# Attention of a two-layer graph network: the gathers' lead over the products is limited to three groups

## The reference, cut to what matters

```python
h = (x @ W.T).reshape(n, H, D)
h_src, h_dst = h[src], h[dst]
alpha = einsum(h_src, a_src) + einsum(h_dst, a_dst)
enc = relu(edge_attr @ edge_W.T + edge_b).reshape(-1, H, D)
alpha = alpha + sum(enc * h_dst, axis=-1)
alpha = where(alpha >= 0, alpha, 0.2 * alpha)
ex = exp(alpha - segment_max(alpha, dst)[dst])
attn = ex / max(segment_sum(ex, dst)[dst], 1e-10)
out = segment_sum(h_src * attn[..., None], dst)
```

## Time and profile before

| | us |
|---|---|
| median of three runs | 3056.0 |
| profiled execution, whole | 3057.23 |
| its span, first to last instruction | 3055.5 |
| attention, from the first gather to the last sum | about 914 (1668 to 2582) |
| POOL busy with L1934 in all | 489.5 in 488 gathers |
| TensorE's mean granted clock | 0.826 of full |

### The profile page before, as it was taken

One profiled execution on the slowest core, in us unless ns is written; L12 is line 12 of the kernel. 1 busy time (PEld: TensorE's weight loads), 2 busy tenths in 40 slices (PEclk: granted clock), 3 DMA queues, 4 the chain that ended last, 5 costly groups with the idle time before them and its releaser, 6 DMA issues. The chain is left out here.

```text
span 3055.5 us, 41553 instructions
## 1 busy us (share of the span) xinstructions
PE 2069.6 (68%) x12602; PEld 1559.8 (51%) x12602; DVE 1660.6 (54%) x3320; ACT 817.5 (27%) x2162; POOL 1225.6 (40%) x1222
## 2 busy tenths in 40 slices
PE   3355656555549985899424276777776676996995
PEld 1244444434437764799412155555555554335995
DVE  7344444444447778555566276767776667403222
ACT  6222222222200001233123122323332323432331
POOL 0366666666640000455213455556565651001221
PEclk9677677777769997899756688888888888997998
DMA  2344444444358844222322344444444432300113
GB/s 74 106 153 153 151 153 152 157 151 147 139 167 296 293 166 137 87 72 71 92 87 83 83 120 117 123 115 132 121 127 117 128 112 78 126 9 20 39 36 104
DMA packets 192123, 366.16 MB, mean 120 GB/s; under 512 B 47573, under 2 KB 102632, under 8 KB 191525
## 3 DMA queue, kind: packets, MB, share of 16 engines
q1 hardware_dynamic: 135472, 207.05, 21.0%
q0 software_dynamic: 56160, 156.43, 16.6%
q10 hardware_dynamic: 274, 0.00, 0.0%
HBM read 232.23 MB, written 131.07 MB: 119 GB/s over the span
## 5 line engine op out<-in xcount | busy, mean ns | idle before, releaser
L1934 POOL DMA_INDIRECT att_rows<-hdram,top_ix x488 | 489.5, 1003 | 382.2 <-DVE att_msg L2162 231.0
L756 POOL DMA_INDIRECT mtab<-msgs_rw,msgs_ix x488 | 486.0, 996 | 376.9 <-ACT msgs_rw L718 186.0
L645 PE MATMUL msgs_p_m<-nodes_n,msgs_hott 128*128 x976 | 358.9, 530 | 54.6 <-issue 41.1
L2006 PE MATMUL att_p_acc<-att_msg,att_hot 128*128 128x264 f32 x976 | 307.5, 469 | 94.6 <-issue 45.0
L578 DVE TENSOR_TENSOR msgs_rw<-msgs_p_m,msgs_sorted 128x1024 f32<-128x1024 f32 x122 | 149.3, 1224 | 339.0 <-PE msgs_p_m L645 124.8
L645 PEld LDWEIGHTS msgs_p_m<-nodes_n,msgs_hott 128*128 128x128 f32 x976 | 245.4, 264 | 120.5 <-issue 75.3
L2006 PEld LDWEIGHTS att_p_acc<-att_msg,att_hot 128*128 128x128 f32 x976 | 211.2, 227 | 150.2 <-issue 89.4
L2036 ACT ACTIVATE att_enc<-att_p_z 128x1024 f32<-128x1024 f32 x122 | 124.8, 1023 | 592.2 <-remote 327.1
L2113 DVE TENSOR_TENSOR att_enc<-att_enc,att_p_h 128x1024 f32<-128x1024 f32 x122 | 148.8, 1220 | 242.6 <-remote 210.2
L826 PE MATMUL sums_part<-sums_rows,sums_hot 128*128 128x256 f32 x976 | 223.8, 387 | 32.4 <-DVE sums_hot L801 32.2
L1348 PE MATMUL exp_y<-exp_own,exp_ht 128*128 128x256 f32 x1032 | 239.0, 379 | 2.4 <-issue 2.4
(11 more groups left out here) (376 smaller groups left out, 3576.2 us busy)
## 6 DMA issues: line engine op xcount, KB each, us to landing
sums_rows<-mtab SPq DMA_DIRECT2D x122, 520.0 KB, 4.6
etab<-msgs_et SPq DMA_DIRECT2D x122, 288.0 KB
att_hz<-etab SPq DMA_DIRECT2D x122, 288.0 KB
first_w<-in_L_ffn_w SPq DMA_DIRECT2D x16, 512.0 KB
ffn0x_w<-in_L_ffn_w SPq DMA_DIRECT2D x16, 512.0 KB
ffn_w<-in_L_ffn_Wd SPq DMA_DIRECT2D x8, 1024.0 KB, 10.6
mtab<-msgs_rw,msgs_ix POOLq DMA_INDIRECT x488
att_rows<-hdram,top_ix POOLq DMA_INDIRECT x488
```

Source lines behind the costliest of these rows:

```text
L645: last = T.matmul(p_m[g % 2][:, q, :], hott[g % 2][:, q, :], node, start=True, stop=True)
L756: nc.gpsimd.indirect_dma_start(mtab, bass.IndirectOffsetOnAxis(ap=ix[:, g, q:q + 1], axis=0), rw[g % RS][:, q, :], None).then_inc(s_free[g ...
L1934: nc.gpsimd.indirect_dma_start(rows[:, g % RS, q, :], None, hdram, bass.IndirectOffsetOnAxis(ap=ix1[:, g, q:q + 1], axis=0)).then_inc(s_ro ...
L2006: last = T.matmul(p_acc[g % 2][:, 0:HW], hot[g % 2][:, q, :], msg[g % 2][:, q, :], start=(q == 0), stop=(q == G - 1))
```

## The change

POOL waits for DVE as well. Before the gathers of group g >= 3 it waits until `products` of group g - 3 has run (`s_prod` is counted up by line 2113), so group g's gathers are issued no earlier than after product g - 3. The wait for the ring slot stays as it was. The unused count `s_go` goes up from g = 3 on instead of from g = 12 on.

```diff
             for g in range(NG):
                 if g >= RS:
                     pool.wait_ge(s_msg, g - RS + 1)
+                if g >= 3:
+                    pool.wait_ge(s_prod, g - 2)
                     pool.sem_inc(s_go, 1)
                 for q in range(G):
                     nc.gpsimd.indirect_dma_start(
```

## The result

Over 20 runs of each kernel the median went from 3055.66 to 3042.53 us; the ratio is 0.9957, 95% interval 0.9942 to 0.9973. That is 13 us faster where 24.7 were forecast. Single runs lay between 3037 and 3076 us before (one of 7329 us aside) and between 3021 and 3051 us after, so two single profiles can't be compared to within 10 us. The profiled execution after took 3045.77 us, its span is 3044.0, the mean granted clock 0.819.

A forecast was written before the change was run, and what follows sets the result against it. The prediction took PE's results, arriving late at DVE under unbroken gathers, as the bound. Profiled 3057.23 us less 29.3 at the start plus 4.6 at the end gave 3032.5, a median of 3031; likeliest case 3013 to 3049, wider range 2994 to 3060.

The forecast's parts named there:

- What bounds the stage: Attention loop: bound by PE's results reaching DVE late, held up while gathers run without a pause; 2.3 us per gather group.
- Rival 3: Attention start: hold-up isn't the gathers' or they don't limit it; product 2 still near 1736, 3056 to 3061 us; chance 0.08.
- The start, product 1 at 1692 to 1695: Stage start: first 16 gathers run as before, then POOL waits for product 1, taken at 1692, bounds 1688.2 to 1695.2.
- Steps 1 to 7 at 5.75: Stage start, no messages: 3.43 us plus 2.3 for gathers per step, 34.5 in all; product 7 at 1726.5, not 1753.78.
- Steps 7 to 12: Stage start, with messages and gathers: 7.06 us a step, 35.3 in all; product 12 at 1761.8 in place of 1791.09.
- The start's sum, 29.3: Product 12 comes 29.3 us earlier than before; by the bounds 37.6 to 18.2 earlier.
- Steady state zero, with 14 us for both signs: Steps 12 to 118: same bursts, 7.06 us a step, no change; 0.13 a step either way, 14 us over 106 steps.
- the forecast's own range: Whole program, likeliest case with chance 0.65: median 3013 to 3049 us, from the start's bounds and the steady state's 14 us.
- The end, +4.6: Stage end: two of the three 4.75 us steps get a gather group of 2.3 us each, 4.6 us later.
- Rows in time: At alphas of each block: gathered rows still arrive in time, 4 us to spare, 11 at 7.06 a step; cost nothing.
- Rival 1: Steady state: gather bursts stay short all along, 6.67 us a step, 41 us more gained, 2990 us; chance 0.12.
- Rival 2: Steady state: POOL restarts where PE begins destinations, 0.5 us more a step, 53 us slower, 3084 us; chance 0.15.

The follow-up runs named there:

- start only: Wait for the product kept only for groups 3 to 11, from group 12 on messages alone as before; against the kernel before: 3097.6 us, ratio 1.0049.
- steady only: Wait for the product only from group 12 on, first twelve groups gathered at once as before; against the kernel before: 3038.9 us, ratio 0.9858.
- the later measurement: The same changed kernel timed again beside its two halves on one chip: 3026.3 us against 3084.3 of the kernel before, ratio 0.9816.
- a lead of one: Group g's gathers wait for product g - 1 instead of g - 3; against the kernel before, on a fast chip: 2705.4 us, ratio 1.0027.

## Why the prediction came out as it did, point by point

- **What bounds the stage.** Right for this chip: products wait for PE's results, late under gathers. The experiment with plain transfers confirms the culprit: without the indirect form the stage loses its 7 us steps at once. Rival 3 (not the gathers) is out. One reading was too narrow. Product 2 waited not for `destinations` alone but also for `encodings(2)` on ACT, which ended at 1734.03, 1.9 us before the product; and ACT had waited for PE's `encoders(2)`, whose row ends at 1684.05, until 1733.01. So the latest result was 49.0 us late, not 36.6:

```profile
1683.04 1.01 PE L1947 MATMUL att_p_z<-top_ewz,att_hz 128*128 128x512 bf16 x2 [5.13 <-issue]
```

PE's own matmuls stood up to 2.63 us apart there with nothing waited for the earlier trace rows. Whether PE is held up itself, or only the news of its results, isn't shown; the ends of its rows are modelled.

- **The start, product 1 at 1692 to 1695.** Right: from product 0 on, 16.0 us where 17.3 were forecast. With the 6.3 us of shift ahead of the stage taken off, products 2, 7 and 12 came at 1694.9, 1729.6 and 1763.7, where before 1700, 1727 and 1762 were named as signs.
- **Steps 1 to 7 at 5.75.** Measured (1735.93 - 1697.11)/6 = 6.47, between the estimate and its bound of 7.07. Steps 7 to 12 took 6.81, forecast 7.06.
- **The start's sum, 29.3.** 27.4 in the profiled pair, so the size was right there. In time of the whole program it was another thing: the start's wait alone made it 13 us longer, and beside the other wait at best some 13 us shorter. A faster start isn't kept as a term of its own; what follows it changes too.
- **Steady state zero, with 14 us for both signs.** This is the step that doesn't hold: "In both kernels DVE gives POOL exactly one group for one step ... So I expect the same bursts and 7.06 a step." The count argument is right and doesn't fix the bursts. The same count gave 92 products in 700 us in start only and 103 in steady only. In the profiled pair the step went from 7.07 to 7.14, +7.8 us, inside the 14; in the later measurement the half that acts only there brought 45 us, three times that bound. The sum's net had the right sign and about twice the measured 13 us. That it came no further off is partly luck: the pair's 11.5 us are the start's 27.4 less 7.8, 1.8, and 6.3 us in code that didn't change, and the later measurement gave 58, more than the 43 at the favourable end of the forecast's own range (3056 less 3013).
- **The end, +4.6.** +1.8 from product 118 on; the last three steps took 15.6 us in place of 14.2 ((2542.6 - 2527.0), from the last and first start), 1.4 us more, where two groups of gathers at 2.3 us each had been counted.
- **Rows in time.** Right: L2129 never waited for the gathered rows in the profile after. At a lead of one, on a chip where POOL is the bound, the first block waited 6.57 us, and 3.13 with the old lead.
- **Rival 1** (bursts stay shorter, 6.67 a step) is nearest to what steady only did: 6.84 from product 12 to 118. Its mechanism isn't borne out, since start only has more and shorter bursts and is the slowest. **Rival 2** (wrong point in the step, 53 us slower) has its sign refuted by the 45 us that steady only gained: releasing at the product is the better point, or the shorter lead is the better lead.

## What to carry to other kernels

When a transfer's issue slows another engine, count on the whole pattern of bursts and not on the average per group: the same supply gave steps of 6.84 and 7.57 us on one chip, by when it was released and by the start that went before. Test the parts of a throttle apart, and don't add them up unchecked; the part that was meant (no burst of 48 at the start) cost 13 us alone and was worth some 13 at best beside the other. And time a kernel that leans on indirect gathers on more than one chip before reading a mechanism off one trace: on three of the chips met here the effect that this change eases wasn't seen.

## What the hardware showed that I had not expected

- One program, two speeds: 3056 and 3084 us in two measurements, 2698 to 2702 us on three other chips. Many rows last the same on both kinds: gather 1003 ns and 1028, product 1220 and 1219, PE's L1348 in a stage without indirect DMAs 379 and 379. The whole difference of the two profiles, 355 us, lies in the parts that have indirect DMAs: 117 us up to product 0 (1674.7 against 1557.6), which has the stage of message rows in it, and 240 from product 0 to 118; the rest takes 515.2 and 517.2. Within the attention PE's rows do differ: L2006 takes 469 ns against 411, at a granted clock of 0.86 against 0.98 in the long stretch (748 and 568 us long), of which PE was busy 539.9 and 485.5. On the slow chip with plain transfers the clock was 0.99 too, so the lower clock goes with the hold-ups and not with the chip; what it costs by itself no run shows. The stage of message rows with its 488 indirect scatters shows the mark of the attention, 117.4 us of waiting for the unnamed sender, which is gone on the other chip. The row of DVE's L578 from the groups of instructions up to the attention stage (to 1668 and to 1545 us), before and then on the other chip:

```profile
L578 DVE TENSOR_TENSOR msgs_rw<-msgs_p_m,msgs_sorted 128x1024 f32<-128x1024 f32 x122 | 149.3, 1224 | 339.0 <-PE msgs_p_m L645 124.8 <-remote 117.4 <-issue 96.5
```

```profile
L578 DVE TENSOR_TENSOR msgs_rw<-msgs_p_m,msgs_sorted 128x1024 f32<-128x1024 f32 x122 | 149.4, 1225 | 287.6 <-PE msgs_p_m L645 243.7 <-DMA mtab<-msgs_rw,msgs_ix 43.9
```

- On a slow chip 48 plain transfers from POOL ran at 340 GB/s beside PE without delaying it (product 2 came 6.1 us after product 0), while beside 48 indirect ones product 2 came 61.2 and 62.1 us after it, and one result of PE was 49.0 us late.
- POOL's plain transfer of 128 rows takes 537 ns of its time, the indirect one 1003 (means over 488).
